# A two-layer decoder kernel: another order of scores, values, loads and row work in its two attention stages

## The reference

```python
x = _layernorm(x + _L0_attn_ref(x, ...))           # causal self attention, 16 heads of 16
x = _layernorm(x + _L0_xattn_ref(x, ctx_768, ...)) # cross attention, 1024 keys
x = _layernorm(x + _L0_ffn_ref(x, ...))            # soft mixture of experts
x = _layernorm(x + _L1_attn_ref(x, ...))           # causal self attention
x = _layernorm(x + _L1_xattn_ref(x, ctx_768, ...)) # cross attention
x = _layernorm(x + _L1_ffn_ref(x, ...))            # x + self attention of a norm, then x + experts of a norm
# every attention:
att = jax.nn.softmax(einsum('bhqd,bhkd->bhqk', q, k) / sqrt(hd) [, causal mask], axis=-1)
y = einsum('bhqk,bhkd->bhqd', att, v);  return y @ Wp + bp
```

## Time and profile before

| | us |
|---|---|
| median of three runs | 2875.1 |
| the runs | 2868.8 to 2877.04 |
| the profiled execution | 2872.66 |
| its span, first to last instruction | 2870.9 |
| stage `first`, first shift to the last group's sums | 61.8 to 805.3 |
| stage `second`, likewise | 1373.2 to 2372.8 |
| PE busy, weight loads busy | 2526.0 (88%), 1449.9 (51%) |
| DVE, ACT, POOL busy | 1494.8 (52%), 1330.3 (46%), 444.9 (15%) |

### The profile page before, as it was taken

The page is one execution under the profiler, slowest core; times in us unless marked ns, Lnnn a source line. Parts: engine busy times, 40 slices in busy tenths (PEclk is TensorE's granted clock), DMA queues, the critical chain, the costliest instruction groups (busy, mean ns, idle before and its releaser), DMA issues. The chain is left out here.

```text
span 2870.9 us, 47221 instructions
## 1 busy us (share of the span) xinstructions
PE 2526.0 (88%) x15793; PEld 1449.9 (51%) x15794; DVE 1494.8 (52%) x4176; ACT 1330.3 (46%) x2833; POOL 444.9 (15%) x687
## 2 busy tenths in 40 slices
PE   6999999999869889997899999999987994499991
PEld 3555544444334456675456544444444553266661
DVE  2555877888544500023555788777745654222224
ACT  2655466667744412111455567666664551022220
POOL 4222221101100000000123212202122001400004
PEclk8999999999999999999899999999998995599996
DMA  7544534233000022114644533242132317311103
GB/s 222 160 134 137 141 85 103 52 78 78 1 1 0 1 95 93 62 48 141 178 131 127 144 93 93 60 107 85 47 94 83 97 51 249 128 33 33 33 29 94
DMA packets 153825, 259.89 MB, mean 91 GB/s; under 512 B 22713, under 2 KB 96705, under 8 KB 149441
## 3 DMA queue, kind: packets, MB, share of 16 engines
q1 hardware_dynamic: 150544, 248.81, 29.9%
q0 software_dynamic: 3072, 8.39, 0.9%
HBM read 180.71 MB, written 81.53 MB: 91 GB/s over the span
## 5 line engine op out<-in xcount | busy, mean ns | idle before, releaser
L1444 ACT ACTIVATE second_p<-psum 128x512 f32<-128x512 f32 (+3 forms) x1024 | 461.5, 522 | 250.4 <-PE psum L1286 246.9
L1444 ACT ACTIVATE first_p<-psum 128x512 f32<-128x512 f32 (+3 forms) x768 | 366.7, 548 | 180.0 <-PE psum L1286 177.2
L1536 DVE TENSOR_REDUCE second_max_parts<-psum 128x1 f32<-128x512 f32 x512 | 323.0, 684 | 72.5 <-PE psum L1263 70.7
L1536 DVE TENSOR_REDUCE first_max_parts<-psum 128x1 f32<-128x512 f32 x512 | 323.0, 684 | 62.6 <-PE psum L1263 61.2
L1532 DVE CUSTOM_DVE_ANT_0 second_masked<-psum,mask_qk 128x384 f32<-128x384 f32 (+3 forms) x512 | 229.3, 488 | 198.1 <-PE psum L1263 168.0
L1298 PE MATMUL psum<-second_p,second_v_aug 128*32 128x512 f32 (+3 forms) x2048 | 236.0, 533 | 8.7 <-ACT second_p L1444 8.3
L1263 PE MATMUL psum<-second_k,second_q 64*128 64x512 f32 (+3 forms) x1024 | 201.0, 390 | 40.1 <-DMA second_k<-a_k_parts 27.4
L1276 PE MATMUL psum<-second_q,second_k 64*128 64x512 f32 (+3 forms) x1024 | 224.1, 434 | 3.3 <-DVE second_max_parts L1536 1.0
L1286 PE MATMUL psum<-second_shift_T,choose 64*128 64x512 f32 (+3 forms) x1024 | 196.9, 380 | 0.0
L1298 PE MATMUL psum<-first_p,first_v_aug 128*32 128x512 f32 (+3 forms) x1536 | 185.6, 555 | 10.5 <-ACT first_p L1444 10.5
L1276 PEld LDWEIGHTS psum<-second_q,second_k 64*128 64x128 f32 x1024 | 97.4, 186 | 186.0 <-ACT second_p L1444 78.1
(11 more groups left out here) (337 smaller groups left out, 3759.2 us busy)
## 6 DMA issues: line engine op xcount, KB each, us to landing
first_k<-c_k_parts SPq DMA_DIRECT2D x64, 256.0 KB, 4.7
second_q<-a_q_parts SPq DMA_DIRECT2D x128, 128.0 KB, 2.9
second_k<-a_k_parts SPq DMA_DIRECT2D x128, 128.0 KB, 2.9
second_k<-c_k_parts SPq DMA_DIRECT2D x64, 256.0 KB, 4.8
first_q<-a_q_parts SPq DMA_DIRECT2D x64, 128.0 KB, 2.9
first_k<-a_k_parts SPq DMA_DIRECT2D x64, 128.0 KB, 2.9
c_k_parts<-first_held SPq DMA_DIRECT2D x16, 512.0 KB, 3.0
first_q<-c_q_parts SPq DMA_DIRECT2D x64, 128.0 KB, 4.4
```

The costliest lines, as they stand in the source:

```text
L1444: evacuated(act.activation(probs[tile % 2][:, 2 * h + p, q0:SEQ], bank[:, q0:SEQ], ACT.Exp, scale=scale), event)
L1536: evacuated(v.reduce_max(max_parts[n % 2][:, h, p, qt, k0 // BANK:k0 // BANK + 1], bank[:, 0:width], axis=AX_X), event)
```

## The change

A step of a self layer (`layer.causal`) becomes scores (t, 0), unit, scores (t, 1), unit, values t-1. The last two bodies of each stage (`n + 2 >= groups`), which have no units, get the same order, in cross layers too. Other cross bodies keep their values between the halves. The turn of group n-1 comes after the second half of step 1 everywhere. `further` issues the load of group n+3 ahead of its vload. In stage `second` the scaled rows of slots 8 to 10 come one step later with one REST more, and their xturns a step after them; those of slot 11 move from step 0 of body 35 to its step 3, with the projections behind them in bodies 36 and 37, and the apply of slot 7 moves from the end of body 33 into body 34. In stage `first` the slot rows of body 20 come one step later.

```diff
--- before.py
+++ after.py
@@ -767,6 +767,20 @@
             at += cost
         return out
 
+    def values(of):
+        if of:
+            plan.append(("values", *of))
+            if of[1] == layer_of(of[0]).key_tiles - 1:
+                plan.append(("drain", of[0], 0))
+
+    def further(n):
+        if n + 1 < groups:
+            plan.append(("augment", n + 1, 0))
+        if NB <= n + 3 < groups:
+            plan.append(("load", n + 3, 0))
+        if n + 3 < groups:
+            plan.append(("vload", n + 3, 0))
+
     def body(n):
         units, own = [], [(x, COST.get(x[0], 300)) for x in pieces.get(n, ())]
         if 0 <= n + 2 < groups:
@@ -782,32 +796,31 @@
             plan.extend(x[0] for x in units)
             return
         if n == groups:
-            last = layer_of(n - 1).key_tiles - 1
-            plan.extend([("values", n - 1, last), ("drain", n - 1, 0), ("turn", n - 1, 0)])
+            values((n - 1, layer_of(n - 1).key_tiles - 1))
+            plan.append(("turn", n - 1, 0))
             plan.extend(x for x, _ in own)
             return
         layer, own = layer_of(n), stream_of(own)
         steps = layer.key_tiles
         for t in range(steps):
+            before = (n, t - 1) if t else (n - 1, layer_of(n - 1).key_tiles - 1) if n else None
             plan.append(("scores", n, (t, 0)))
-            share(units, 2 * t + 1, 2 * steps)
-            if t:
-                plan.append(("values", n, t - 1))
-            elif n:
-                plan.extend([("values", n - 1, layer_of(n - 1).key_tiles - 1), ("drain", n - 1, 0)])
-            if t == 1:
-                if n:
-                    plan.append(("turn", n - 1, 0))
-                if n + 1 < groups:
-                    plan.append(("augment", n + 1, 0))
-                if n + 3 < groups:
-                    plan.append(("vload", n + 3, 0))
-                if NB <= n + 3 < groups:
-                    plan.append(("load", n + 3, 0))
+            if n + 2 < groups:
+                share(units, 2 * t + 1, 2 * steps)
+                if not layer.causal:
+                    values(before)
+                if t == 1:
+                    further(n)
             if t == steps - 1 and n + 1 < groups:
                 plan.append(("shift", n + 1, 0))
             plan.append(("scores", n, (t, 1)))
             share(units, 2 * t + 2, 2 * steps)
+            if n + 2 >= groups or layer.causal:
+                values(before)
+            if t == 1 and n:
+                plan.append(("turn", n - 1, 0))
+            if t == 1 and n + 2 >= groups:
+                further(n)
             if n + 1 < groups and t < 3:
                 plan.extend([("chain", n + 1, 2 * t), ("chain", n + 1, 2 * t + 1)])
             share(own, t + 1, steps)
@@ -2388,7 +2401,7 @@
             else:
                 pieces[GROUPS * (slot + 1)] = output_pieces(c0, slot) + rms_pieces(slot)
         pieces[GROUPS * BATCH + GROUPS - 1] += [("slot_stats", 0, 0), ("slot_root", 0, 0)]
-        pieces[GROUPS * BATCH + GROUPS] = [REST] + slot_pieces()
+        pieces[GROUPS * BATCH + GROUPS] = [REST, REST] + slot_pieces()
         soft_ctx = ctx.enter_context(ExitStack())
         c.rows = soft_ctx.enter_context(nc.sbuf_tensor("soft_rows_kept", [P, NT, D], F32))
         c.xT = soft_ctx.enter_context(nc.sbuf_tensor("soft_xT_kept", [P, DK, T], F32))
@@ -2430,11 +2443,14 @@
             whole = front_pieces(a2, slot, "x")
             pieces[first + 1] = output_pieces(c1, slot - BATCH)
             if b < BATCH - 1:
-                pieces[first + 2] = [REST, REST] + scaled_rows(slot) + whole[:5]
-                pieces[first + 3] = whole[5:]
+                pieces[first + 2] = [REST] * 3 + scaled_rows(slot) + whole[:4]
+                pieces[first + 3] = whole[4:]
             else:
-                pieces[first + 3] = scaled_rows(slot) + whole[:5]
-                pieces[first + 4] = whole[5:]
+                apply = pieces[first + 1].pop()
+                pieces[first + 2] = [REST, apply, REST, REST]
+                pieces[first + 3] = [REST, REST] + scaled_rows(slot) + whole[:3]
+                pieces[first + 4] = whole[3:7]
+                pieces[first + 5] = whole[7:] + pieces[first + 5]
             first += NG
             pieces[first + (b < BATCH - 1)] = output_pieces(a2, slot)
         fills = [(rows_dram[at:min(at + T, TILES * P), :], x_rows[0:min(T, TILES * P - at), :], rows_filled)
```

## The result

| | before | after |
|---|---|---|
| median of four runs, us | 2874.65 | 2838.66 |
| lowest to highest | 2868.8 to 2877.04 | 2836.75 to 2840.86 |
| the profiled execution (its span) | 2872.66 (2870.9) | 2837.0 (2835.2) |

The ratio is 0.9878, with a 95% interval from 0.9861 to 0.9896: 36 us faster, where 41 were forecast (2834). The time lies in the range. The parts do not fit as well as their sum: four terms came out 4 to 7 us worse than forecast, and one, the turn, 13 us better, so that the sum owes its fit in part to luck.

What follows compares the result with a forecast made beforehand. PE sets the pace in the attention stages, by how long it is held between starts; DVE bounds some bodies. Terms summing to -41.1 from the profiled 2872.7 us gave 2831.6, with 2.4 for the median 2834; range 2808 to 2857.

Steps and rivals of the forecast that it cites:

- part 1: Last two bodies of each stage: both score halves ahead of the values remove the wait for ACT; -14.6 us.
- part 2: Eleven self bodies without pieces: the new order removes small waits of weight loads, 0.55 us each; -6.0 us.
- part 3: Self bodies with splits: the unit after scores (t, 1) waits for its bank without the values' cover; +11.5 us.
- bodies 14 and 15: Self bodies making maximum scores for a cross group, both stages: bounded by DVE, so no change; 0 us.
- part 4: Bodies 4, 7 and 11: the load ahead of the vload ends most of PE's waits for keys; -5.8 us.
- part 5: Body 35 of stage second: the load wait goes, the xturn's wait and half its clock loss stay; -12.2 us.
- part 6: Slots 8 to 10, bodies 22, 26 and 30: rows a step ahead of xturns shorten waits; -12.5 us.
- Rival 4: More latency loops open: turns leave 30 cross bodies' loop, self bodies save 0.8, lost cover costs nothing; 2810 us, chance 0.18.
- the first (the cover decides): Self bodies with units: units behind scores (t, 1) wait longer, 1.4 us a body, 64 in all; 2887 us, chance 0.04.
- The second (the gaps are banks): Last bodies and self bodies without pieces: gaps come from banks, the order gives nothing; 2855 us, chance 0.10.
- The third: Loads stay late because something else holds SP; part 4 and part 5 give only the clock; 2850 us, chance 0.09.
- The fifth: Thirty cross bodies: the turn's bank, taken after the second unit, delays the next unit 0.3 us each; 2843 us, chance 0.08.

Runs made afterwards that it cites:

- mixed version: Changed kernel with values between the halves except in a2's self bodies without pieces, and slot 11's rows, xturns and projections a step apart: 2811.7 us, ratio 0.9800.
- best version: Like the mixed version, but xturns of slots 8 to 10 two steps behind their rows: 2814.7 us, then 2809.2 in five rounds, ratio 0.9783.

## Why the prediction came out as it did

| step of the prediction | forecast | measured in bodies |
|---|---|---|
| part 1, last bodies | -14.6 | -13.8 |
| part 2, self bodies without pieces | -6.0 | -1.3 |
| part 3, self bodies with splits and other pieces | +11.5 | +16 |
| bodies 14 and 15 of both stages | 0 | +7.2 |
| turn behind the second half | 0 | -13 |
| part 4, the load first, bodies 7 and 11 | -5.8 | -6.2 |
| part 5 and body 37 (bodies 35 to 38) | -13.7 | -14.4 |
| part 6, rows of slots 8 to 10 | -12.5 | -8.5 |
| the rest: clock and loads at the stages' starts, bodies 16 and 20, ends | 0 | about -2 |
| sum | -41.1 | -36 (spans: -35.7) |

The measured column separates the two orders by differences between kernels that differ in one of them: the turn by the kernel with the turn alone, the late values by the changed kernel against the ones that have the turn late and the values between. Where bodies are touched by both, the turn's 0.18 and the late values' part are taken out of the other terms.

**Part 1** was right in size and cause. The step came to 2.10 to 2.13 where 2.17 was forecast; ACT ends it, one of the two candidates named. The Trainium skill ("Perfetto Trace Analysis", section "Optimization Strategy") says that a repeating gap can mean too little PSUM or SBUF for the next tile. That was not so here: the same 7 banks serve the shorter step.

**Part 2** failed. Its upper bound came from body 8, whose bare steps seemed 0.8 us shorter than body 42. I read this as splits that cover waits, which no order removes where there is nothing to cover with; no run tests that reading. The row on which the part rested shows waits of weight loads, and the loads wait alike in both orders: 3.8 us in body 42 of the changed kernel and 4.0 with the values between the halves, at 11.27 and 11.19 us for the body. Body 32 alone is clearly shorter (0.86), but it holds three values instead of four, and body 46, which holds four instead of three, gives 0.68 back (9.65 against 8.97). So even the 1.3 of the table is 0.6 when body 46 is read with it. The lower bound, 0, was nearly the value to take.

**Part 3** named the right wait: it is in the rows at 216.72, its size in steps 1 and 2 of body 8 is 0.35 and 0.40, where 0.34 was worked out for step 2, and it goes when the values take their place ahead of the unit again. Two things were left out. I held step 3 safe because the shift stands between its halves; in fact the scores behind the shift now wait for the split's second activation, 0.3 us in each body with a split there, since the values no longer stand ahead of the shift. And small losses of a tenth or two come in bodies with value pieces, too. So a body with two to four splits loses 0.8 to 1.3 (most, 1.3, with three splits and nothing else), and the sum is 16, inside the bounds of 7 and 20.

**Bodies 14 and 15** were put at nothing, "DVE's". That they are DVE's is just why they lose. Values and pieces now stand together: in step 1 of body 15 values, turn and split take 1.00 + 0.49 + 1.81 us, and in that time DVE gets no maximum scores. Then four units come within a step, eight banks, and wait for it. DVE's timeline in the changed kernel begins a run of eight maxima only after an idle stretch behind the split:

```profile
352.23 4.87 DVE L1549 TENSOR_REDUCE first_max_parts<-psum 128x1 f32<-128x512 f32 x8 [0.83 <-PE psum L1276]
```

and PE's waits of body 15 are those of its units for DVE (0.9 us in 2 times before):

```profile
PE psum L1276 <- DVE first_max_parts L1549: 2.1, 5, 0.7
PE psum L1289 <- ACT first_p L1457: 0.8, 2, 0.5
```

Over the body DVE waits for PE's maximum scores 4.4 us in 4 times, where it was 1.9 in 3. With the values ahead of the unit body 15 is at 23.4, with them between the halves at 22.8. An engine that is full is not safe from a change of order on the engine that feeds it.

**The turn** was priced at 0, since DVE is full in cross bodies, with bounds of -9 and +9 for the 30 of them. There the gain is 0.17 each, 5 us, inside the bounds; the 44 self bodies, for which the prediction had no term at all, give another 8. Together they are the largest error. PE was in truth held in every step of a cross body by a bank, 0.24 us ahead of the unit behind scores (t, 0), without a gap that the busy column shows (PE counts as busy for 23.83 of 24.40 us there). A turn ahead of scores (2, 0) gives ACT time where PE would wait; one ahead of scores (1, 1) stands where no one waits. Rival 4 had 0.3 us each for 30 cross bodies.

**Parts 4 and 5** were right in size, but for body 4 of stage second: part 4 left it a wait of about 1.0, and it waits 2.2. In part 5 the cause was told half: SP stood at the vload because of the augment behind the apply, and the change mends this twice, by the load ahead of the vload and by the apply a body later. Each alone is enough. The wait of the xturns of slot 11 was forecast at 4.1 and is 3.88; the clock then fell for 6.8 us, 2.4 of loss by its 0.65.

**Part 6**: the waits came out near the 1.6 and 0.8 of the prediction (1.49 and 0.89), the first of them in part by luck: the prediction speaks of a step of about 2.9 us and then takes off 3.2, for which it shows no row; with 2.9 it would have been 1.9. And in the kernel before the clock had been low for 6.8 us in body 22 and for 3.4 in 26, not alike, and in the changed kernel it fell for 3.4 us in body 26 all the same: pair 26 and 27 gives 1.7, not 4.6.

The signs named for the new profile: body 31, to its last scores, is at 18.0 us (18.5 forecast), body 8 at 17.5 (17.2), the cross body at 24.3. Bodies 42 to 44 were to be at 10.8 and are at 11.3 to 11.4. Body 35 was to be near 20 with the xturn's wait in it; it is at 11.3, and the wait is in body 36 (24.0).

The rivals: the first (the cover decides) is refuted in its size, and its point was not reached: 1.15 a body, against some 0.35 in the mean of the self bodies other than 14 and 15, and 0.5 with these. The second (the gaps are banks) is refuted for part 1; its number holds for part 2, while no run shows that banks are the reason. The third is refuted by the rows of the load. The fourth had the right place with the wrong size, and left out the self bodies. The fifth had the sign wrong.

## What to carry to other kernels

An order that puts work ahead of a wait also takes it from where it covered another wait: for each instruction moved, look for who now stands without cover behind it, and where a piece (here the turn) could be put to cover what waits in every step. PE shown busy all through can still be held at each step; compare the distances between starts of the same two instructions in places where nothing can hold them, and the difference is the wait. When two edits aim at one wait, try each alone: here either took away the same 12 us, and the edit that gave the change its name was the one that cost time.

## What the hardware showed

One thing was not expected: how much the granted clock can do after the same short wait. In body 4 of stage second PE waits 1.4 us for keys in the mixed version and 1.6 in the one with the values between the halves. These are the busy times of the body in the first and then in the second of these kernels:

```profile
1419.80:1432.60 12.80, 11.23 (x122) 6.91 (x122) 8.61 (x41) 7.14 (x18) 0.74 (x1) 1.00 0.41 112
1422.50:1440.60 18.10, 16.40 (x122) 9.64 (x122) 9.52 (x44) 7.23 (x19) 0.73 (x1) 0.65 0.30 81
```

In the second the clock fell to the lower level (1.2 GHz instead of 2.4) in the middle of the body and stayed there into the next one, which took 25.0 us instead of 21.6: 8.6 us in two bodies, from waits that differ by 0.2. The best version was run twice with a profile, and PE waited 1.4 us in body 4 both times: the body took 15.19 us once, with the clock low for 6.8 us, and 17.84 the other time, with the clock low for 17.1. So a wait of some 1.5 us costs itself or several times as much, and single terms of 2 to 8 us in a sum like this one can't be checked by the total of a few runs; the bodies without waits can. What decides it is open.
